# A graph kernel's sort: bias parts on nine partitions, the scatter's first part of 64 columns, and another order of products and word operations

## The reference

```python
def _L0_gnn_ref(edge_index, edge_type, embeddings, weights, biases):
    dest, src = edge_index[0], edge_index[1]
    out = embeddings
    for l in range(L):                                        # L = 3
        X = jnp.einsum('ne,ref->rnf', out, weights[l])        # nine products a layer
        msg = X[edge_type, src] + biases[l][edge_type]
        hidden = jax.ops.segment_sum(msg, dest, num_segments=N)
        if l + 1 < L:
            hidden = jax.nn.relu(hidden)
        out = hidden
    return out
...
x = _layernorm(x + _L0_gnn_ref(edge_index, edge_type_9, x, weights, biases), axis=-1)
x = _layernorm(x + _L1_gnn_ref(x, beta, edge_index), axis=-1)   # attention over the same edges
```

## Time and profile before

| what | value |
|---|---|
| median of 3 runs | 3996.73 us (3995.7 to 3997.86) |
| profiled execution, its time | 4001.13 us |
| its span, first to last instruction | 3999.4 us |
| busy over the span: PE, DVE, POOL, ACT | 73%, 68%, 66%, 20% |
| end of the edges' load, start of the first operation on them | 9.62 us |
| first scatter, last scatter | 77.36 us, 505.09 us |
| first and last instant of the put products | 172.48 us, 513.05 us |
| first gather | 526.18 us |

### The profile page before, as it was taken

One profiled execution on the slowest core, in us unless ns is written; L12 is line 12 of the kernel. 1 busy time (PEld: TensorE's weight loads), 2 busy tenths in 40 slices (PEclk: granted clock), 3 DMA queues, 4 the chain that ended last, 5 costly groups with the idle time before them and its releaser, 6 DMA issues.

```text
span 3999.4 us, 57212 instructions
## 1 busy us (share of the span) xinstructions
PE 2913.7 (73%) x14372; PEld 1860.7 (47%) x14372; DVE 2714.3 (68%) x9164; ACT 801.6 (20%) x1939; POOL 2632.2 (66%) x2787
## 2 busy tenths in 40 slices
PE   6999966676777678777777777787774444447998
PEld 2555544444444445444444444554443333335776
DVE  6488875676667668776767665777664333337999
ACT  0688801000100010100100010001000000004665
POOL 4777767777777775777777777577777777770000
PEclk6999988898889989998899888999885555557999
DMA  2300012342433332333343333323333111113554
GB/s 83 135 2 2 2 42 73 88 108 73 107 88 103 73 108 83 80 85 103 83 106 79 103 86 79 115 73 75 87 78 73 53 53 53 53 53 115 193 190 135
DMA packets 374776, 337.04 MB, mean 84 GB/s; under 512 B 262929, under 2 KB 326985, under 8 KB 374342
## 3 DMA queue, kind: packets, MB, share of 16 engines
q0 software_dynamic: 88000, 158.81, 16.4%
q1 hardware_dynamic: 83110, 113.84, 8.3%
q10 hardware_dynamic: 203360, 60.73, 6.2%
HBM read 226.02 MB, written 130.74 MB: 89 GB/s over the span
## 4 chain that ended last, share of the span: by engine, by line
POOL 46%; PE 26%; issue 17%; DVE 7%; DMA 3%; ACT 1%; SPq 0%; DVEq 0%; POOLq 0%; ACTq 0%
POOL region L1054 46%; PE ps L1148 9%; PE ps L1193 3%; PE ps L1276 3%; PE ps L1202 3%; PE ps L1237 3%; DMA region<-x_of_type_in_layer,arrays 2%; PE ps L1304 2%; PE ps L1099 1%; DVE region L792 1%; DVE region L665 1%; DVE region L599 1%; PE ps L1279 1%; DVE region L600 1%; PE ps L1079 1%
## 5 line engine op out<-in xcount | busy, mean ns | idle before, releaser
L1054 POOL DMA_INDIRECT region<-x_of_type_in_layer,arrays x1612 | 1523.3, 945 | 552.3 <-issue 477.9
L1193 PE MATMUL ps<-region,oh 128*102 x5040 | 1112.6, 324 | 789.9 <-SPq L918 490.4
L1193 PEld LDWEIGHTS ps<-region,oh 128*102 128x102 f32 x5040 | 920.9, 204 | 1340.6 <-issue 1078.6
L1202 PE MATMUL ps<-region 128*128 128x510 f16 x4200 | 1355.0, 410 | 182.6 <-ACT ps L1362 138.7
L594 DVE TENSOR_SCALAR oh<-iota_w,arrays 128x102 f32<-128x102 f32 x2528 | 730.1, 290 | 1051.6 <-PE ps L1193 1026.3
L1054 POOL DMA_INDIRECT region<-x_of_type,arrays x806 | 763.7, 948 | 265.5 <-issue 263.0
L665 DVE TENSOR_TENSOR region<-region,ps 102x128 f32 x2520 | 713.9, 283 | 3.1 <-issue 2.8
L1202 PEld LDWEIGHTS ps<-region 128*128 128x128 f16 x4200 | 433.6, 104 | 249.5 <-issue 197.8
L1373 ACT COPY region<-ps 128x510 f32<-128x510 f32 x155 | 89.8, 579 | 2246.4 <-PE ps L1202 2245.9
L599 DVE TENSOR_SCALAR region<-ps,arrays 128x640 f16<-128x640 f16 x844 | 459.6, 545 | 0.0
L1036 POOL DMA_INDIRECT scattered_edges<-region x332 | 322.4, 971 | 155.6 <-issue 106.3
(11 more groups left out here) (243 smaller groups left out, 1621.3 us busy)
## 6 DMA issues: line engine op xcount, KB each, us to landing
x_of_type_in_layer<-region SPq DMA_DIRECT2D x90, 576.0 KB
edge_counts<-region ACTq DMA_DIRECT2D x155, 255.0 KB
arrays<-edge_counts SPq DMA_DIRECT2D x40, 960.0 KB, 5.0
region<-x_of_type_in_layer,arrays POOLq DMA_INDIRECT x1612, 2.5
edge_absent<-region ACTq DMA_DIRECT2D x155, 127.5 KB
region<-edge_absent SPq DMA_DIRECT2D x40, 480.0 KB, 3.8
region<-x_of_type,arrays POOLq DMA_INDIRECT x806, 2.5
x_of_type<-x0st SPq DMA_DIRECT2D x51, 192.0 KB, 1.9
```

What stands on the lines that cost most here:

```text
L1054: pool.indirect_dma_start(out=grow[:, t % GR * D:(t % GR + 1) * D], out_offset=None, in_=xts[l], in_offset=bass.IndirectOffsetOnAxis(ap=gi ...
L1193: mm = pe.matmul(ps[0:RB, 6 + n % 2, t * D:(t + 1) * D], oh[:, u % U, 0:RB], grow[:, bass.ds(at[u % PAIRS], D)], start=True, stop=True)
L1202: mm = pe.matmul(ps[:, c, 0:CW], cl[:, q % CR, c * P:(c + 1) * P], cr[:, q % CR, :], start=False, stop=False, skip_group_check=True)
```

## The change

It has six parts.

- **Bias.** SP loads nine rows of the first layer's bias (9 by 128) in place of all biases to all partitions. GpSimd splits these (five operations on 9 by 128 values in place of twelve on 96 or 32 by 1152). Three small DMAs write the three parts to DRAM, and when all are there a fourth reads them back as three rows of 1152. The other layers' biases and beta come behind that. The bias product now has three rows instead of 96.
- **Constants.** `choose` is cast on ScalarE, not on GpSimd.
- **Warm-up.** TensorE multiplies zeros 24 times (512 columns) before the counting.
- **Words.** The five operations on the edges' words move from behind "bases" to just behind the comparisons.
- **Places.** `place` runs over 64, 268 and 476 columns. GpSimd may start when the first 64 are there and waits once more before the next. The operations that lead to "ends" and "past" move from behind the first part's places to behind all places.
- **First-layer products.** Two stand ahead of the product of totals (L1123), six between it and the bucket products, sixteen between the 268-column ones, sixteen between the 476-column ones, and 35 follow. GpSimd's waits for the stores of X and its register loads now stand ahead of its wait for "rows".

```diff
+    CA = 64
+    WARM = 24
+    FIRST_X = 8
...
         def _(dve):
...
             for b in range(NK):
                 nc_.tensor_scalar(eq[:, b, :], keyb, float(b), None, ALU.is_equal).then_inc(s_eq, 1)
+
+            step(nc_.tensor_scalar(posi, posi, float(MB - 1), -float(RB), ALU.min, ALU.mult))
+            step(nc_.tensor_tensor(posi, srci, posi, ALU.add))
...
             step(nc_.tensor_copy(base_h[0:H, :], digit_i[0:H, :]), "bases")
-            step(nc_.tensor_scalar(posi, posi, float(MB - 1), -float(RB), ALU.min, ALU.mult))
-            step(nc_.tensor_tensor(posi, srci, posi, ALU.add))
...
-            place(0, CP, 0)
...
+            place(0, CA, 0)
+            cells(0, CA, "first_cells")
+            place(CA, CP - CA, NK)
+            cells(CA, CP, "cells")
+            place(CP, EP, 2 * NK)
...
-            place(CP, EP, NK)
             dve.wait_ge(s_fill, 16)
+            dve.wait_ge(s_later, 32)
...
         def _(sp):
...
-            sp.dma_start(bias[:, :], biases.rearrange("l r f -> (l r f)").partition_broadcast(P)).then_inc(s_bias, 16)
+            sp.dma_start(bias_s[0:R, :], biases[0]).then_inc(s_bias, 16)
...
-            sp.dma_start(betab[:, :], beta.partition_broadcast(P)).then_inc(s_const, 16)
+            sp.wait_ge(s_pool, BIAS_PARTS)
+            for n in range(3):
+                sp.dma_start(bias_parts[n].rearrange("(r d) -> r d", r=R), bias_x[n][0:R, :]).then_inc(s_parts, 16)
+            sp.wait_ge(s_parts, 48)
+            sp.dma_start(bias_t, bias_parts).then_inc(s_parts, 16)
...
         def _(pool):
...
-            pool.wait_ge(s_d, marks["cells"])
+            pool.wait_ge(s_d, marks["first_cells"])
             for t in range(CP):
+                if t == CA:
+                    pool.wait_ge(s_d, marks["cells"])
                 pool.indirect_dma_start(
...
+            pool.wait_ge(s_d, marks["ends"])
+            again = values_of(pool, again_made, 1, 16 * EARLY, 1)[0]
+            for u in range(X0):
+                pool.wait_ge(s_x0d[u], 16 * (-(-(NB * XC - u) // X0)))
             pool.wait_ge(s_d, marks["rows"])
-            again = values_of(pool, again_made, 1, 16 * EARLY, 1)[0]
...
         def _(pe):
+            pe.wait_ge(s_d, marks["zeros"])
+            for n in range(WARM):
+                pe.matmul(ps[:, 7, :], zerob[:, 0:P], zerob[:, :], start=True, stop=True)
...
+            pe.wait_ge(s_const, 64)
+            turn_nodes(0)
+            pe.wait_ge(s_parts, 64)
+            for q in range(2):
+                first_x(q)
+            pe.wait_ge(s_d, marks["counts"])
+            pe.matmul(ps[:, 0, 0:NK], ones[0:NK, :], tot_diag[0:NK, :], start=True, stop=True).then_inc(s_t, 1)
+            for q in range(2, FIRST_X):
+                first_x(q)
+            pe.wait_ge(s_d, marks["bases"])
+            pe.wait_ge(s_pool, CONSTANTS)
+            pe.wait_ge(s_choose, 1)
             for b in range(NK):
-                bucket(0, CP, b, b)
-            pe.wait_ge(s_const, 80)
-            pe.wait_ge(s_pool, BIAS_PARTS)
-            turn_nodes(0)
+                bucket(0, CA, b, b)
             for b in range(NK):
-                bucket(CP, EP, b, NK + b)
+                bucket(CA, CP - CA, b, NK + b)
                 if b % 2:
-                    first_x(b // 2)
-            for q in range(NK // 2, NB * XC):
+                    first_x(FIRST_X + b // 2)
+            for b in range(NK):
+                bucket(CP, EP, b, 2 * NK + b)
+                if b % 2:
+                    first_x(FIRST_X + NK // 2 + b // 2)
+            for q in range(FIRST_X + NK, NB * XC):
                 first_x(q)
...
         def _(act):
+            act.wait_ge(s_pool, CONSTANTS - 2)
+            act.copy(choose[0:2 * NK, :, :],
+                     chosen[0:2 * NK, :].unsqueeze(2).to_broadcast([2 * NK, NK, P])).then_inc(s_choose, 1)
```

More of the change, by code:

```diff
@@ L223, in gnn_program @@
         twice, chosen, tot_diag = part(NK), part(NK), part(NK)
-        bias_d = part(RF)
-        bias_x = [part(RF // 2, BF16) for _ in range(3)]
+        bias_s, bias_d = part(D), part(D)
+        bias_x = [part(D // 2, BF16) for _ in range(3)]
         used[0] = MB * D
@@ L425, in _ @@
                 nc_.tensor_scalar(eq[:, b, :], keyb, float(b), None, ALU.is_equal).then_inc(s_eq, 1)
+            step(nc_.tensor_scalar(posi, posi, float(MB - 1), -float(RB), ALU.min, ALU.mult))
+            step(nc_.tensor_tensor(posi, srci, posi, ALU.add))
+            step(nc_.scalar_tensor_tensor(out=word, in0=dsti, scalar=float(R), in1=typei,
+                                          op0=ALU.mult, op1=ALU.add))
+            step(nc_.scalar_tensor_tensor(out=word, in0=posi, scalar=float(1 << ROW_BIT), in1=word,
+                                          op0=ALU.mult, op1=ALU.add))
+            step(nc_.tensor_scalar(word, word, 1.0, None, ALU.add))
             tot, til, te, ts, off = (sm[:, i, :] for i in range(4, 9))
@@ L482, in place, with cells @@
                 step(nc_.tensor_scalar(posi[:, lo:lo + n], pos[:, lo:lo + n], -RAISE, None, ALU.add))
-            place(0, CP, 0)
[L486 to L491, removed]
+            def cells(lo, hi, mark):
+                ti, tj = (t.bitcast(I32)[:, lo:hi] for t in tmps[0:2])
+                step(nc_.tensor_scalar(ti, posi[:, lo:hi], P - 1, None, ALU.bitwise_and))
+                step(nc_.tensor_scalar(tj, posi[:, lo:hi], 7, None, ALU.arith_shift_right))
+                nc_.tensor_copy(pay[:, lo:hi, 0], word[:, lo:hi])
+                step(nc_.scalar_tensor_tensor(out=pay[:, lo:hi, 1], in0=ti, scalar=float(NT), in1=tj,
+                                              op0=ALU.mult, op1=ALU.add), mark)
+            place(0, CA, 0)
[3 more added lines that the diff above has]
+            place(CP, EP, 2 * NK)
             late = sm[:, 10, :]
@@ L1021, in _ @@
[L1021 to L1027, removed]
@@ L1028, in _ @@
-            finished(nc_.memset(ones_3[0:H3, :], 0.0))
-            for n in range(3):
-                finished(nc_.memset(ones_3[n * NK:n * NK + 1, :], 1.0))
+            finished(nc_.tensor_copy(bias_x[0][0:R, :], bias_s[0:R, :]))
+            finished(nc_.tensor_tensor(bias_d[0:R, :], bias_s[0:R, :], bias_x[0][0:R, :], ALU.subtract))
+            finished(nc_.tensor_copy(bias_x[1][0:R, :], bias_d[0:R, :]))
+            finished(nc_.tensor_tensor(bias_d[0:R, :], bias_d[0:R, :], bias_x[1][0:R, :], ALU.subtract))
@@ L1069, in _ @@
             mm.then_inc(s_t, 1)
-            pe.wait_ge(s_d, marks["counts"])
-            pe.matmul(ps[:, 0, 0:NK], ones[0:NK, :], tot_diag[0:NK, :], start=True, stop=True).then_inc(s_t, 1)
             def bucket(lo, n, b, k):
-                if b == 0:
-                    pe.wait_ge(s_d, marks["bases"])
                 if k >= 2:
@@ L1136, in turn @@
                         mm.then_inc(s_t, 1)
[L1138 removed]
+            pe.wait_ge(s_bm, 3 * NK)
             for c in range(4):
```

35 lines of the change are left out of this document (16 added, 19 removed).

## The result

The changed kernel takes 4048.97 us (median of 20 executions), the kernel before 3997.59 us (20 executions): by the medians the change makes it 51 us slower; the prediction was 3975 us. The ratio is 1.0111, 95% interval 1.0099 to 1.0123, over the executions within 1.5% of each kernel's fastest, which leaves out six of the changed kernel's, from 4058 to 4792 us. Of the other 14, one took 3996.29 us and 13 took 4041 to 4050 us; the one has a mean granted clock of 0.848 over the execution, the 13 have 0.835 to 0.840.

What follows compares the result with a forecast made beforehand. TensorE's end of put was taken to set the first gather, the scatter staying hidden. TensorE's 20.6 us plus 0.9 us gave 21.5 us less: 4001.1 to 3979.6 us profiled, 3975 us median; 8-in-10 range 3968 to 4019 us.

Steps and rivals of the forecast that it cites:

- TensorE from 48 us on: TensorE's bucket stages and 35 last first-layer products: through at 145.6 us in place of 166.2, 20.6 us less.
- five steps low, eleven high: 268-column stage on TensorE: five steps at 2.95 us, eleven at 1.69, with transposes 34 us, until 82 us.
- the 64-column stage: First 64 columns of `place`: 0.38 us a block number, 12.2 us in all (bounds 7 and 25).
- The cast: Ahead of VectorE's chain to "bases": GpSimd's cast of 3.59 us goes to ScalarE, 1.6 us less.
- the comparisons: VectorE's 32 comparisons ahead of "bases": 10 us instead of 19.4, 9.3 us less.
- the counting hidden by the words: VectorE's 3.25 us wait for TensorE's counting, filled by 4.3 us of word operations: 3.25 us less.
- the bound of 7 us for a slow counting: TensorE's counting at 1.2 GHz: 7 us more than comparisons and words together; 0 taken, 7 us as bound.
- The first copy of `place`: End of VectorE's chain after "bases": moves from 49.44 to 35.8 us.
- The register load's 0.9 us: GpSimd ahead of the first gather: register load and store waits moved before the indices' wait, 0.9 of 1.8 us off.
- a clock that stays low in both bucket stages: Rival on TensorE: 1.2 GHz through 268- and 476-column stages, put 23 us later, 4018 us; chance 0.34.
- Rise with the 476-column products: Rival on TensorE: clock rises only with 476-column steps, four low, twelve high; 3996 us, no change; chance 0.11.
- late bias parts: Rival: bias parts or weights land late, product of totals waits 4 to 10 us; 3979 to 3986 us; chance 0.05.

Runs made afterwards that it cites:

- the pairs: Changed kernel, bias product still on three rows, order bias, bias, product, product in place of single first-layer products; 3994.39 us, ratio 0.9984 against the kernel before.

## Why the prediction was wrong

**The step that failed** is the one on TensorE from 48 us on. It took a low step of 268 columns as one of 476 with shorter bucket products (2.95 us) and the tail as 0.85 us a product, and so priced the bias product on three rows at nothing. The runs show 3.24 and 1.11 us, 0.30 us more for each of 75 products, 22 us. The second half of that step, "five steps low, eleven high", failed with the same product: no step was high in the changed kernel, all but four were with 96 rows. By stage, the changed kernel against the same kernel with 96 rows: until the first 64-column product 40.48 against 34.40 us, the 268-column stage 52.9 against 32.0, the 476-column stage 65.2 against 33.6, the tail 40.8 against 29.7, the small products behind it 8.0 against 6.1, together 72 us with 0.2 in the 64-column stage. Of these 22 us are the longer steps, by the estimate above; the other 50 come with the clock.

**The other steps.** With 96 rows they can be read off. The cast (L427 in 0.58 us), the comparisons (9.36 us against 10) and the counting hidden by the words held; the bound of 7 us for a slow counting did not come into play: some 3 us of it were slow, with the warm-up and without, and the words hid them. The first copy of `place` came at 34.8 us (35.8 forecast), the 64-column stage took 11.3 us (12.2), the first scatter came at 48.20 us (50). The clock rose at 56.5 us, after some four low steps, where 62 us and five were forecast, a low step took 2.95 us and a high one 1.69, as worked out. The put began at 147.0 us (152). The register load's 0.9 us: from the put's end to the first gather it is about 12 us, and was 13. That the time of this kernel meets the 3975 us is luck: its put came 5 us sooner than forecast, and the 4.4 us by which a profiled execution was taken to be longer than the median were 0.9 us here (3976.01 against 3975.12). In the changed kernel itself the first copy of `place` fell short, 41.0 us: six first-layer products at the low clock, 2.0 us each, stood in front of it, which the prediction had not priced.

**The rivals.** The first, a clock that stays low in both bucket stages, is what happened; it was priced at 4018 us, 31 us too low, mostly since its steps too had the bias product at its old length (22 us) and no low clock ahead of the bucket products (6 us). It gave two reasons together, 268 columns and three rows. The first is refuted by the run with 96 rows, which has the same bucket products; the second was right, though for the clock only, and not priced for the length of a step. By its own steps the change would turn to a loss with a clock low to about 113 us, not "some 100": the 21.5 us of gain pay for eleven more low steps of 268 columns and for some five of 476. It leaned also on the Trainium skill's "TensorE: Matmul & The Clock Gate", section "A second HAM failure mode: psum-queue depth-cycling"; the run with 96 rows cycles through the same PSUM banks, and its clock is up from 56.5 us, so that rule is not what decided here. Rise with the 476-column products and late bias parts did not occur.

The page that bore on the change was another: the Trainium skill's "TensorEngine Tiling (Array Packing)", section "Tiling Modes", says that changing the tiling mode drains TensorE. If a product of 3 or of 64 rows is in another mode than one of 128, which no run shows by itself, the rows agree: they put 0.10 us on a change between bucket products at 2.4 GHz, and none on 96 beside 128. The same pause stood in the trace of before, between the bucket products of 128 and 64 rows, unread.

**What stays open.** That the three-row product costs the time is shown in both directions; how it keeps the clock low is not shown to the end. Pauses (the pairs) and rows in use (64 against three) both seem to move the instant at which the clock rises; how they are weighed against each other was not measured. In the pairs two first-layer products also stand back to back, which the run does not separate from the fewer pauses.

## What to carry to other kernels

A matmul of few rows among products of 128 rows is not free because its columns are few: read the start-to-start times of neighbouring products, and where they exceed the columns, pad the contraction with zero rows until the pause is gone (here 96 rows) or put products of one kind behind each other. When an edit changes an operand's partitions, price the instruction that reads it anew, at both clocks. When the clock decides the sign, a busy share of 100% in the profile does not say that products follow without pauses; compare the step with its columns. And when one path has become shorter, look which one ends last: here it became the scatter.

## What the runs showed of the hardware

- TensorE was busy for 143.15 of 143.20 us at a granted clock of 0.50: pauses between products do not show as idle time there.
- A bias product of three or of 64 rows made a first-layer product 0.30 us longer at 2.4 GHz (1.11 against 0.81 us), one of 96 rows did not, whether its rows held values or zeros.
- Of that 0.20 us lie between the float32 product and the next bias product (0.85 us from start to start, 0.65 with 96 rows) and 0.10 between the bias product and the float32 product (0.26 against 0.17 us). With 96 rows the weights were loaded 0.32 and 0.16 us ahead of their products, with three rows at their start.
- One kernel, that with 64 rows, took 3990 to 4047 us in ten executions.
- With the same work on both, VectorE's 32 comparisons took 19.40 us beside GpSimd's split of the bias in one profiled execution, and 9.04 us in another, where GpSimd's first operation took 8.56 us in place of 1.22.
- The granted clock read 1.00 while nine products of 404 columns took 0.32 us each; later ones took 0.17.
